# Sending each token tile's rows one block sooner in GpSimd's order

## What is computed

```python
xs, z = split(x @ W_in.T)                        # 512 channels each
xc = silu(causal_conv4(xs) + conv_b)             # depthwise, 4 taps
a  = softplus((xc @ W_x.T)[:, :32] @ W_dt.T + b_dt)
x  = layernorm(x + x + (xc * a * silu(z)) @ W_out.T)
# experts: sigmoid scores, best 2 of 4 groups, best 4 experts, weights normed to 2.5
y  = sum_e weight_e * (silu(x @ Wg_e.T) * (x @ Wu_e.T)) @ Wd_e.T
y += (silu(x @ Ws_g.T) * (x @ Ws_u.T)) @ Ws_d.T
out = layernorm(x + x + y)
```

## Time and profile before

| | |
|---|---|
| median of 3 runs | 683.1 us |
| the runs | 671.84, 683.1, 683.78 us |
| the profiled execution, span from first to last instruction | 679.4 us |
| TensorE busy | 554.9 us (82%) |
| VectorE busy | 415.7 us (61%) |
| ScalarE busy | 373.9 us (55%) |
| GpSimd busy | 321.7 us (47%) |

### The profile page before, as it was taken

The page is one execution under the profiler, slowest core; times in us unless marked ns, Lnnn a source line. Parts: engine busy times, 40 slices in busy tenths (PEclk is TensorE's granted clock), DMA queues, the critical chain, the costliest instruction groups (busy, mean ns, idle before and its releaser), DMA issues.

```text
span 679.4 us, 11679 instructions
## 1 busy us (share of the span) xinstructions
PE 554.9 (82%) x3127; PEld 467.5 (69%) x3127; DVE 415.7 (61%) x1120; ACT 373.9 (55%) x961; POOL 321.7 (47%) x361
## 2 busy tenths in 40 slices
PE   6998999999999998856380887978878878778594
PEld 5684868787878776645270886968768768768583
DVE  5895989898989897734240553333323456566496
ACT  4768686767676755423220565645545545555554
POOL 3502123666767677665356444446346345345320
PEclk9999999999999999887595898979779789789797
DMA  7974130424242322694153375545335757667397
GB/s 197 278 228 153 63 125 28 153 80 149 84 146 88 115 80 93 216 369 141 61 185 117 114 238 186 167 126 155 117 117 159 236 184 235 218 189 233 110 343 263
DMA packets 70150, 111.06 MB, mean 163 GB/s; under 512 B 12260, under 2 KB 53477, under 8 KB 69576
## 3 DMA queue, kind: packets, MB, share of 16 engines
q1 hardware_dynamic: 56856, 74.36, 35.3%
q0 software_dynamic: 12672, 35.67, 14.5%
q10 hardware_dynamic: 560, 0.27, 0.1%
HBM read 61.63 MB, written 49.69 MB: 164 GB/s over the span
## 4 chain that ended last, share of the span: by engine, by line
PE 44%; another core or an unknown queue 17%; DVE 15%; ACT 12%; issue 9%; DMA 3%; ACTq 1%; DVEq 0%
PE psum L737 5%; PE psum L738 4%; PE psum L739 4%; PE psum L796 4%; PE psum L1008 3%; PE psum L874 3%; PE psum L771 3%; PE psum L998 2%; PE psum L999 2%; PE psum L1000 2%; PE psum L982 2%; DMA gu_hi_buf<-w_hi_now 2%; ACT y_out L1318 2%; DVE xc L1468 1%
## 5 line engine op out<-in xcount | busy, mean ns | idle before, releaser
L669 POOL DMA_INDIRECT x_buf<-row,row_id x128 | 129.0, 1008 | 75.3 <-DVE row_id L1775 39.1
L2074 DVE TENSOR_TENSOR e_act<-g_act,psum 128x512 f32<-128x512 f32 x36 | 24.6, 684 | 139.6 <-ACT g_act L1303 121.6
L998 PE MATMUL psum<-ew_gu_hi,t_hi 128*128 x286 | 91.3, 319 | 0.4 <-issue 0.4
L1303 ACT ACTIVATE g_act<-psum 128x512 f32<-128x512 f32 x36 | 21.8, 606 | 120.5 <-remote 96.1
L999 PE MATMUL psum<-ew_gu_lo,t_hi 128*128 x286 | 87.4, 305 | 0.0
L1000 PE MATMUL psum<-ew_gu_hi,t_lo 128*128 x286 | 87.0, 304 | 0.0
L661 POOL TENSOR_TENSOR m<-xc,zs 128x512 f32<-128x512 f32 x32 | 41.4, 1314 | 95.9 <-DVE shift L1546 57.0
L726 POOL DMA_INDIRECT y_buf<-y_out,y_ids x56 | 55.2, 985 | 57.5 <-ACT y_out L1318 37.8
L1468 DVE SCALAR_TENSOR_TENSOR xc<-psum,cw_taps,xc 128x511 f32<-128x511 f32 (+2 forms) x96 | 70.7, 738 | 6.5 <-ACT halo_x L1134 5.0
L1008 PE MATMUL psum<-ident,e_act 128*128 128x128 f32 x143 | 27.6, 325 | 52.2 <-DVE e_act L2074 50.1
L726 POOL DMA_INDIRECT y_buf<-row,y_ids x40 | 39.9, 998 | 48.5 <-ACT row L1318 36.7
(11 more groups left out here) (259 smaller groups left out, 1471.6 us busy)
## 6 DMA issues: line engine op xcount, KB each, us to landing
tiles_in<-x_buf SPq DMA_DIRECT2D x143, 144.0 KB
y_pair<-y_buf SPq DMA_DIRECT2D x20, 512.0 KB
y_in<-y_buf SPq DMA_DIRECT2D x12, 512.0 KB, 6.9
xT<-in_x_T SPq DMA_DIRECT2D x8, 512.0 KB
xtok<-in_x_tok SPq DMA_DIRECT2D x8, 512.0 KB
gu_hi_buf<-w_hi_now SPq DMA_DIRECT2D x8, 512.0 KB, 3.2
x_buf<-pad_row SPq DMA_DIRECT2D x17, 144.0 KB
raw_gu<-in_wg_T SPq DMA_DIRECT2D x16, 128.0 KB, 3.4
```

The costliest lines, as they stand in the source:

```text
L669: nc.gpsimd.indirect_dma_start(out=x_buf, out_offset=bass.IndirectOffsetOnAxis(ap=row_id[t % ROWS][:, b, k:k + 1], axis=0), in_=row[t % RO ...
L998: pe.matmul(o, t_hi[par][:, k, r], w_hi, start=k == 0, stop=False)
```

## The change

The same DMAs are issued, in another order. Before, GpSimd's part of tile t had block 3 of tile t-3 and block 0 of tile t-2 behind the products of chunks 2 and 3, block 1 behind the products of chunks 0 and 1, and block 2 behind the halo products. After it, blocks 0 and 1 of tile t-2 stand behind the products of chunks 2 and 3 (ahead of the wait for the norm), block 2 behind the products of chunks 0 and 1, and block 3 behind the halo products. In tile 6 blocks 0 and 1 of tile 4 are sent together, as they were before by `tile` and the first line of `last_tile`; that line falls away.

```diff
                 at_least(pool, "y_done", PAIRS * t + 1)
                 gate_product(t, range(2, KI))
-                if t > 2:
-                    send(t - 3, range(3, SUB))
                 if t > 1:
-                    send(t - 2, range(0, 1))
+                    send(t - 2, range(0, 2))
                 if t == NT - 2:
                     return
                 at_least(pool, "norm_ready", t + 1)
                 gate_product(t + 1, range(0, 2))
                 if t > 1:
-                    send(t - 2, range(1, 2))
+                    send(t - 2, range(2, 3))
                 halo(t + 2)
                 if t > 1:
-                    send(t - 2, range(2, 3))
+                    send(t - 2, range(3, SUB))

             def last_tile(t):
-                send(t - 3, range(1, 2))
                 at_least(pool, "norm_ready", t)
                 gate_product(t, range(0, KI))
                 send(t - 3, range(2, SUB))
```

## The result

| | before | after |
|---|---|---|
| median of 20 runs each | 682.75 us | 689.24 us |
| lowest and highest | 671.84, 687.14 | 681.97, 701.04 |
| profiled execution | span 679.4 | 691.4, span 689.7 |
| TensorE busy | 554.9 us | 553.8 us |

The change makes the kernel slower by 6.5 us in the medians (1.0%). The ratio taken over undisturbed executions alone, those not in the slower state that some executions fall into, is 1.017, 95% interval 1.0126 to 1.0215, which would be 8.6 to 14.7 us. Executions of one kernel lie up to 19 us apart, so the times give the sign and the rough size of the cost, and the trace has to give its parts. The forecast was 691 (675 to 698).

What follows compares the result with a forecast made beforehand. TensorE's own work was taken to bound each tile. Span 679.4 plus 8.0 (four tiles at 2.0, direct delay 0) gives 687.4; with 3.7 from span to median, 691.1 us, range 675 to 698.

Steps and rivals of the forecast that it cites:

- What bounds it: First half, tiles 2 to 5: TensorE's own work sets the 34.17 us period, so only what makes TensorE wait counts.
- Part 1: Tiles 2 to 5: sends delay GpSimd's products of chunks 0 and 1 by 0.8 to 1.5 us, covered; cost 0.
- Part 2: Tiles 2 to 5: sends beside VectorE's norm string slow it from 2.45 to 5.14 us; TensorE waits 2.0 each, 8.0 us.
- Tile 6: Same eight sends stay beside its norm string, so nothing taken; at best its 2.0 us wait goes away.
- Tile 7: Its norm string before, 7.58 us with sends all through, priced the upper end at 4.5 us a tile.
- the heavy end: Upper end for tiles 2 to 5: norm strings as slow as tile 7's, 4.5 us times four, 18.2 us.
- The sum: Whole kernel: span 679.4 + 8.0 = 687.4 us; median forecast 691.1 us, 1.2% slower.
- A: Norm strings need more than eight sends to be slow, so tile 6 loses its wait: faster, 681.1 us; chance 0.17.
- B: Tile 6's norm string is slow for a reason of its own, so no change: 683.1 us; chance 0.15.
- C: Tiles 2 to 5: GpSimd's late product blocks VectorE's subtraction, both reading SBUF; 2.0 us, 685.1 us; chance 0.08.
- D: Tiles 2 to 5: norm strings become those of tile 7, 701.3 us; chance 0.12.
- What the earlier trace held against the forecast: Run of sends from 310.03: a dependent VectorE routing instruction started 9.6 us behind the first send with no idle time.

Runs made afterwards that it cites:

- kernel with four kinds: Kernel before plus, beside one string each: SyncE DMAs (tile 2), held-back indirect sends (3), GpSimd ordinary DMAs (4), block 1 (5); 675.8 us.
- block-1 kernel: Kernel before with only block 1 of tile t-2 sent ahead of the norm in tiles 2 to 5, block 3 unmoved; 699.78 us, ratio 1.0218.
- pause kernel: Changed kernel plus eight small chained GpSimd products between the sends of blocks 0 and 1 in tiles 2 to 5; 693.97 us, ratio 1.0127.

## Why the prediction was right, step by step

**What bounds it.** Right: TensorE was full before, and every wait added to it lengthened the tile. The stretch 177.52 to 213.76, tile 4 after, is 36.24 us, the predicted period 36.2, and the granted clock is 1.00 as before:

```profile
177.52:213.76 36.24, 34.41 (x155) 26.14 (x154) 30.12 (x92) 23.85 (x44) 22.53 (x27) 1.00 0.33 109
```

**Part 1.** The cost of 0 is nearly right, but the products did not move by the way that was worked out. The prediction has the sends hold up the products of chunks 0 and 1, by 0.8 to 1.5 us. In tile 4 the sends were over at 196.99, and the products waited another 1.57 us for the norm, which Part 2 itself had made late; they start 2.5 us later against their tile (7.50 less the lag of 4.99). The prediction had not carried its second part into its first. The cover held all the same: the next products started 0.41 behind the send ahead of them and were done 1.8 us ahead of VectorE's m at 218.07. In tile 2 it did not quite: three sends of 1.89 to 1.95 us made them end at 145.44, and m started at 145.55, 0.36 behind the end of sp, which it follows by 0.03 in tile 4. The working had allowed one long send of 1.61.

**Part 2.** Right in mechanism, place and size: strings of 4.31 to 5.21 for 5.14, and tile steps of 2.02 to 2.32 for 2.0. Two deviations cancel, which is luck. The waits for sh of tiles 2 to 5 are 1.16 + 2.20 + 1.83 + 2.07 = 7.26 us, 0.7 less than the 8.0. Most of the other 1.3 of the 8.53 is no wait: TensorE's own busy time grew from 34.17 us to 34.41 in tile 4 and in tile 5, and its first matmuls behind a wait take 1.99 for 1.89. The sentence on which the part rests is too wide, though: it says that the string was slow wherever GpSimd was sending through it. Tile 3 of the kernel with four kinds had sends from 0.5 us ahead of its string to its end, and it took 2.45. What the slow strings share is a run over 8 us old.

**Tile 6.** Taken at nothing; right, 1.84 for 2.01. **Tile 7** was used only as a price: its string is 1.4 us shorter after the change, but the waits of the matmuls with m ahead of it rose from 1.8 to 3.2. As a price it was read too high. By itself this string takes 3.39 us, so the heavy end would have been 7.58 - 3.39 - 0.59 = 3.6 us a tile, 14.4 in place of 18.2.

**The sum.** 8.0 predicted in tiles 2 to 5, 8.53 measured; the 10.3 of the two spans holds 0.84 from ahead of the change and 1.1 from behind the row numbers of tile 6. The median moved by 6.5, the ratio of the runs makes 8.6 to 14.7; the term of 8.0 is borne out by the trace, and the times can't tell it from either.

**The rivals.** A (more than eight sends are needed) fell: strings of tiles 2 to 5 are slow with eight. But its cause is half there: behind a run of twelve VectorE's wait for TensorE's results was far longer than behind one of eight (7.45 us for 1.74). B (tile 6 has a reason of its own) fell with the block-1 kernel. C missed by 0.4 us: the product ends at 201.06, the subtraction starts at 201.43, so nothing was lost here; the pause kernel had VectorE 3.0 us late by it in each of tiles 3 to 5. D (tile 7's strings) did not come.
The Trainium skill (SBUF — State Buffer, "Who interferes with whom") has the loser of such a meeting block fully; by that rule the subtraction would take 1.22 + 2.51 = 3.7 us at most, and it was measured at 4.21. The trace agrees with the blocking, and was 0.5 us above the sum. The trace also shows where the 0.5 may lie: a send stood beside the subtraction's start (199.19 to 200.15), and the product followed it at once. From the subtraction's start to the product's end it is 3.12 us, and 3.12 + 1.22 = 4.34. The six-element sum started at 236.84, also beside a send and 0.69 us ahead of the product, and ended with the product at 240.04.

What the earlier trace rows held against the forecast stays open. A run 9.6 us old did not delay that instruction, though in the tiles late starts begin at about 8. The same instruction of the kernel after started at 328.64, again with no idle time before it.

## What to carry to other kernels

Before moving indirect sends on GpSimd, look at what lies beside them on the other engines: on all but one of the chips a run of eight or more delayed dependent chains of tiny instructions, and other engines behind it, and this cost more than the direct delay of the moved work. Break long runs up with other GpSimd work where there is room (it gained 0.8% in the kernel before, and nothing in the change), and check what the displaced GpSimd products then meet on VectorE. An anomaly in one tile of the trace (here tile 6) is the best price list for a change that brings its neighbourhood to the other tiles.

## What the runs showed of the hardware

**Instructions start late beside long runs of indirect DMAs.** A dependent VectorE instruction in such a run started 0.35 to 1.2 us late where it otherwise starts with no gap, from about 8 us behind the first send on; ScalarE and VectorE, waiting for TensorE, started up to 7 us late. In the second half the same picture is far larger, and I had not looked there. ScalarE, kernel before:

```profile
332.65 0.60 ACT L1303 ACTIVATE g_act<-psum 128x512 f32<-128x512 f32 x1 [13.48 <-remote]
...
373.08 0.60 ACT L1303 ACTIVATE g_act<-psum 128x512 f32<-128x512 f32 x1 [20.80 <-remote]
```

A run of sixteen sends ended at 329.96 and one of twenty (sixteen to x_buf, four to y_buf) at 370.3; both times ScalarE woke 2.7 to 2.8 us behind the end, though the last of TensorE's matmuls that it waited for the first time began at 319.52. The expectations call this late counts, and that can't be all of it. TensorE beside the second of these runs, kernel before; the last three are the products of one expert, and the program has no wait between them:

```profile
353.68 0.28 PE L1024 MATMUL psum<-ew_d_hi,a_lo 128*128 x1
353.80 0.28 PE L1022 MATMUL psum<-ew_d_hi,a_hi 128*128 x1
354.82 0.28 PE L1023 MATMUL psum<-ew_d_lo,a_hi 128*128 x1 [0.74 <-issue]
356.93 0.28 PE L1024 MATMUL psum<-ew_d_hi,a_lo 128*128 x1 [1.83 <-issue]
```

Up to 353.80, 8.9 us behind the first send, the matmuls start 0.12 us apart, and then up to 2.1, though no count of a semaphore is waited for. That each engine gets its next instruction late would fit this as well as the slow strings; no run tells it from late counts.

TensorE's waits, kernel before (330 to 679), and then the kernel with ordinary DMAs from GpSimd's queue on the chip of 546.3 us (330 to 542), where the sends to x_buf run unbroken from 280.14 to 339.36:

```profile
PE psum L1008 <- DVE e_act L2074: 50.1, 14, 13.3
```

```profile
PE psum L990 <- DMA tiles_in<-x_buf: 1.1, 3, 0.5
```

The first half takes nearly the same time on both kinds of chip (var of tile 7 at 289.58 and, in this kernel, at 284.94). Of the 136.7 us between the two spans 132 lie behind it, where TensorE's granted clock is 0.79 to 0.90 on the one and 0.97 to 1.00 on the other. How much of it the late starts make is not shown: no run broke up the sends of tile 7 or those to y_buf. What holds the instructions up is not shown either. The runs exclude four ordinary DMAs in flight, four ordinary DMAs of GpSimd in the place tried, and the mere presence of four indirect ones; they show that a pause of 2.7 to 2.9 us after four sends removes the effect on the string. The data of eight indirect sends in a row was not tried apart from their issue.

**A send isn't always 0.96 us.** Beside VectorE's large instructions with two inputs in SBUF, single sends took 1.6 to 2.0 us (128.59, 1.89 us, beside the subtraction at 128.38, kernel after).
